# Transposes one unit later and a new order of work on three engines, in the forward stages of a four-layer kernel

## What is computed

```python
# layer 0: attention over channels
att = einsum('bcn,bdn->bcd', q, q)            # the Gram product
x = gamma * einsum('bcd,bdn->bcn', softmax(max(att) - att), q) + x
# layer 1: long convolution with a separable kernel hx (x) hy per channel
x = irfft2(rfft2(x) * rfft2(k)) + x * bias
# layer 2: Haar transform, two weighted channel mixes with soft thresholds
f1 = haar2d(x)
for i in range(2):
    f4 = einsum('bchw,oc->bohw', f1 * v[i], conv_w[i])
    acc = acc + sign(f4) * relu(abs(f4) - tau[i])
x = haar2d(acc, inverse=True) + x
# layer 3: a second long convolution like layer 1
```

## Time and profile before

| | |
|---|---|
| median of 3 runs | 6386.52 us (6386.07 to 6387.25) |
| the profiled execution | 6390.89 us, span 6389.1 us |
| PE busy | 5852.7 us (92%), weight loads 4944.5 us (77%) |
| DVE busy | 3975.6 us (62%) |
| ACT busy | 3883.7 us (61%) |
| POOL busy | 2526.3 us (40%) |
| chain that ended last | PE 85%, ACT 4%, DVE 3%, DMA 3%, issue 3% |
| DMA | 1216.97 MB, mean 190 GB/s |

### The profile page before, as it was taken

The page is one execution under the profiler, slowest core; times in us unless marked ns, Lnnn a source line. Parts: engine busy times, 40 slices in busy tenths (PEclk is TensorE's granted clock), DMA queues, the critical chain, the costliest instruction groups (busy, mean ns, idle before and its releaser), DMA issues.

```text
span 6389.1 us, 154198 instructions
## 1 busy us (share of the span) xinstructions
PE 5852.7 (92%) x47200; PEld 4944.5 (77%) x47200; DVE 3975.6 (62%) x6260; ACT 3883.7 (61%) x6105; POOL 2526.3 (40%) x2436
## 2 busy tenths in 40 slices
PE   5588589999999999999999999999999999999689
PEld 3277268888888888888888888878888887788579
DVE  1033158755886567755786568855786557766866
ACT  0222257755776667755776667755776657755865
POOL 0000045522553245522554245522554235533952
PEclk7599689999999999999999999999999999999789
DMA  6655666576666766666665866667665855534224
GB/s 183 208 179 175 208 191 206 185 238 207 206 207 191 249 186 206 202 214 215 204 207 184 253 191 207 197 215 229 194 206 179 253 173 166 166 116 138 76 85 129
DMA packets 770795, 1216.97 MB, mean 190 GB/s; under 512 B 78854, under 2 KB 475047, under 8 KB 770568
## 3 DMA queue, kind: packets, MB, share of 16 engines
q1 hardware_dynamic: 623112, 945.61, 50.0%
q10 hardware_dynamic: 147456, 268.50, 11.7%
HBM read 808.07 MB, written 405.73 MB: 190 GB/s over the span
## 4 chain that ended last, share of the span: by engine, by line
PE 85%; ACT 4%; DVE 3%; DMA 3%; issue 3%; ACTq 1%; SPq 1%; POOL 1%; DVEq 0%; POOLq 0%
PE ps L467 29%; PE ps L469 14%; PE ps L517 8%; PE ps L485 8%; PE ps L493 7%; PE ps L477 7%; PE ps L445 4%; PE ps L626 4%; PE ps L527 3%; DMA mixed<-x 2%; ACT x L802 1%; DMA pix<-in_x_pix 1%; DVE pix L1046 1%; DVE field L960 1%; ACT ps L847 1%
## 5 line engine op out<-in xcount | busy, mean ns | idle before, releaser
L1078 POOL TENSOR_TENSOR mag<-mag,sgn 128x512 f32<-128x512 f32 x896 | 1037.0, 1158 | 2154.8 <-ACT mag L733 2154.8
L467 PE MATMUL ps<-tab_a,img 128*128 128x256 f32 x4096 | 1288.9, 397 | 108.5 <-ACT mid L759 94.2
L1095 POOL TENSOR_TENSOR split_a<-field,split_a 128x512 fp32r<-128x512 f32 x512 | 650.7, 1271 | 1663.8 <-ACT split_a L785 1663.8
L467 PE MATMUL ps<-tab_b,mid 128*128 128x256 f32 x4096 | 1224.4, 381 | 0.0
L469 PEld LDWEIGHTS ps<-tab_a,img 128*128 128x128 f32 x4096 | 787.1, 192 | 110.1
L469 PEld LDWEIGHTS ps<-tab_b,mid 128*128 128x128 f32 x4096 | 778.9, 190 | 105.5
L467 PEld LDWEIGHTS ps<-tab_a,img 128*128 128x128 f32 x4096 | 663.7, 192 | 197.8 <-ACT mid L759 71.7
L469 PE MATMUL ps<-tab_a,img 128*128 128x128 f32 x4096 | 794.1, 276 | 0.0
L937 DVE TENSOR_TENSOR held<-ps,v_t 128x1024 f32<-128x1024 f32 x448 | 548.5, 1224 | 385.1 <-PE ps L517 385.1
L469 PE MATMUL ps<-tab_b,mid 128*128 128x128 f32 x4096 | 787.5, 274 | 0.0
L952 DVE TENSOR_TENSOR diff<-ps,tau_t 128x1024 f32<-128x1024 f32 x448 | 548.3, 1224 | 299.1 <-ACT ps L724 299.1
(11 more groups left out here) (92 smaller groups left out, 9394.3 us busy)
## 6 DMA issues: line engine op xcount, KB each, us to landing
pix<-in_x_pix SPq DMA_DIRECT2D x256, 512.0 KB, 4.4
mixed<-x ACTq DMA_DIRECT2D x512, 256.0 KB, 3.3
img<-mixed SPq DMA_DIRECT2D x512, 256.0 KB, 3.6
tab_a<-filt SPq DMA_DIRECT2D x1024, 128.0 KB, 3.0
tab_b<-filt SPq DMA_DIRECT2D x1024, 128.0 KB, 3.3
out<-res SPq DMA_DIRECT2D x512, 256.0 KB, 3.1
coef<-res ACTq DMA_DIRECT2D x496, 256.0 KB, 2.4
pix<-in_x_rows SPq DMA_DIRECT2D x128, 512.0 KB, 5.0
```

The source lines that it names most:

```text
L467: nc.tensor.matmul(o_ps, src[:, 0, H * half:H * half + H], tab[:, N - 1::-1], start=True, stop=False)
L1078: nc.gpsimd.tensor_tensor(mag[:, s], mag[:, s], sgn[:, s], ALU.mult).then_inc(c_mult, 1)
L1095: nc.gpsimd.tensor_tensor(split_a[:, 1], src, split_a[:, 0].bitcast(F32), ALU.subtract)\
```

## The change

On PE `turn` no longer closes the step of its own unit. It runs in the next step, behind the Gram and ahead of the row Toeplitz, for the unit before; it waits for the same count of field additions per unit as before. Also on PE, the column Toeplitz and `haar_fwd` change places, in all forward stages. On ACT, where the stage shrinks, the store moves from behind the high piece to between absolute and sign (in the last, draining steps and in the stage that doesn't shrink it stays). On DVE, where the stage shrinks, the low piece moves from the end of the step to behind held, and is of unit n-3 there, not n-2. No instruction is added or taken away.

```diff
--- before.py
+++ after.py
@@ -557,9 +557,9 @@
                         row_products(4, crows[j // 2], j % 2).then_inc(c_mm, 1)
 
                     def turn():
-                        src = crows[j // 2]
-                        pe.wait_ge(c_field, 64 * b + d + CR)
-                        row_turns(6, src, j % 2).then_inc(c_copy, 1)
+                        e = (j - 1) % 4
+                        pe.wait_ge(c_field, 64 * b + d - 1 + CR)
+                        row_turns(6, crows[e // 2], e % 2).then_inc(c_copy, 1)
 
                     def gram_four():
                         e = j - 1
@@ -573,6 +573,8 @@
                         products()
                     if gram and on[1] and not opening:
                         gram_four()
+                    if shrink and on[1] and not opening:
+                        turn()
                     if fwd and on[0]:
                         pe.wait_ge(img_in[j], 16 * (16 * (b + 1) + q) + 16)
                         pe.wait_ge(ftab_in[j], 32 * (16 * (b + 1) + q) + 32)
@@ -584,22 +586,22 @@
                         products()
                     if gram and on[1] and opening:
                         gram_four()
-                    if fwd and on[2]:
-                        pe.wait_ge(f_x1, n - 1 + CR)
-                        pe.wait_ge(f_lo, n - 2 + CR)
-                        haar_fwd(2, x1[:, j % 2]).then_inc(f_mm3, 1)
+                    if shrink and on[1] and opening:
+                        turn()
                     if fwd and on[1]:
                         d1 = j - 1
                         pe.wait_ge(f_mid, n + CR)
                         pe.wait_ge(f_x1, n - 1 + CR)
                         toeplitz(1, mid[:, d1 % 2], tab_b[:, d1 % 4]).then_inc(f_mm2, 1)
+                    if fwd and on[2]:
+                        pe.wait_ge(f_x1, n - 1 + CR)
+                        pe.wait_ge(f_lo, n - 2 + CR)
+                        haar_fwd(2, x1[:, j % 2]).then_inc(f_mm3, 1)
                     if fwd and on[3]:
                         pe.wait_ge(f_hi, n - 2 + CR)
                         pe.wait_ge(f_lo, n - 2 + CR)
                         pe.wait_ge(f_res, n - 3 + CR)
                         haar_halves(3, split_b, s_fwd_half).then_inc(f_mm4, 1)
-                    if shrink and on[0]:
-                        turn()
                     if gram and isinstance(q, int) and q == 16 and j == 0:
                         gram_edge(False).then_inc(gram_done, 1)
                     if fwd and shrink and isinstance(q, int) and q == 16 and j == 1:
@@ -719,10 +721,12 @@
                     n = f0 + 4 * q + j
                     m = 64 * b + 4 * q + j
 
-                    def absolute_and_sign():
+                    def absolute():
                         act.wait_ge(c_scaled, m + 1 + CR)
                         nc.scalar.activation(pair_of_banks(2), held[:].rearrange("p s n -> p (s n)"), ACT.Abs)\
                             .then_inc(c_abs, 1)
+
+                    def sign():
                         act.wait_ge(c_mult, 2 * m + CR)
                         nc.scalar.activation(sgn[:].rearrange("p s n -> p (s n)"),
                                              held[:].rearrange("p s n -> p (s n)"), ACT.Sign).then_inc(c_sign, 1)
@@ -732,9 +736,7 @@
                         act.wait_ge(c_pair, 2 * m + s - 1 + CR)
                         nc.scalar.activation(mag[:, s], diff[:, s], ACT.Relu).then_inc(c_relu, 1)
 
-                    if shrink and on[0]:
-                        absolute_and_sign()
-                        relu(0)
+                    draining = isinstance(q, int) and q == 16
 
                     def store():
                         d = j - 4
@@ -746,12 +748,18 @@
                         tile = last_res[d + 2] if draining and j >= 2 else res[:, d % 2]
                         act.dma_start(dst, tile.rearrange("p a n -> p (a n)")).then_inc(coef_out[d % 2], 16)
 
-                    draining = isinstance(q, int) and q == 16
+                    if shrink and on[0]:
+                        absolute()
+                    if fwd and shrink and on[4] and not draining:
+                        store()
+                    if shrink and on[0]:
+                        sign()
+                        relu(0)
                     if fwd and on[2]:
                         act.wait_ge(f_mm3, n - 1 + CR)
                         act.wait_ge(f_mm4, n - 2 + CR)
                         nc.scalar.activation(split_b[:, 0], halved(ps[:, 2, :]), ACT.Copy).then_inc(f_hi, 1)
-                    if fwd and on[4] and not draining:
+                    if fwd and not shrink and on[4] and not draining:
                         store()
                     if fwd and on[0]:
                         act.wait_ge(f_mm1, n + 1 + CR)
@@ -931,6 +939,11 @@
                     m = 64 * b + 4 * q + j
                     banks = pair_of_banks(2).rearrange(grouped, y=16)
 
+                    def low_piece(unit):
+                        dve.wait_ge(f_hi, unit + 1 + CR)
+                        nc.vector.tensor_tensor(split_b[:, 1], halved(ps[:, 2, :]), split_b[:, 0].bitcast(F32),
+                                                ALU.subtract).then_inc(f_lo, 1)
+
                     if shrink and on[0]:
                         dve.wait_ge(c_mm, m + 1 + CR)
                         dve.wait_ge(c_sign, m + CR)
@@ -938,6 +951,8 @@
                                                 table(v_t, q, j), ALU.mult).then_inc(c_scaled, 1)
                     if fwd and shrink and isinstance(q, int) and q == 16 and j == 3:
                         inverse_halves(64 * b, 0)
+                    if fwd and shrink and on[3]:
+                        low_piece(n - 3)
                     if fwd and on[4]:
                         d = j - 4
                         draining = isinstance(q, int) and q == 16
@@ -967,10 +982,8 @@
                         nc.vector.scalar_tensor_tensor(out=x1[:, d % 2], in0=img[:, d % 4],
                                                        scalar=bias1[:, bass.ds(4 * q + d, 1)], in1=halved(ps[:, 1, :]),
                                                        op0=ALU.mult, op1=ALU.add).then_inc(f_x1, 1)
-                    if fwd and on[2]:
-                        dve.wait_ge(f_hi, n - 1 + CR)
-                        nc.vector.tensor_tensor(split_b[:, 1], halved(ps[:, 2, :]), split_b[:, 0].bitcast(F32),
-                                                ALU.subtract).then_inc(f_lo, 1)
+                    if fwd and not shrink and on[2]:
+                        low_piece(n - 2)
                 quads(dve, 16, 4 if fwd else 1, step)
                 if shrink:
                     dve.wait_ge(c_field, 64 * b + 64 + CR)
```

## The result

The changed kernel took 6316.38 us in the median of four runs (6309.09 to 6321.73), the kernel before 6386.89: a ratio of 0.9888, interval 0.9871 to 0.9905. That is 70 us or 1.1% faster; the forecast was 6325 and 62 us. Its profiled execution took 6313.23 us with a span of 6311.4, against 6389.1.

What follows compares the result with a forecast made beforehand. With a Gram, PE's list and a ring through DVE's field addition both took 6.33 us a unit; without one, the ring bound. Gains of 18 + 36 + 8 = 62 us gave 6325 us, range 6300 to 6350 (0.68).

Steps and rivals of the forecast that it cites:

- The ring: Products, held, absolute, diff, field addition, transposes, next products: 6.33 us a unit; with transposes moved, 5.08 us, up to diff.
- PE's list with a Gram: Stages with a Gram: PE's work in the new order sums to 6.29 us a unit against 6.345, 18 us in all.
- Rival B: Only the stage without a Gram and the openings gain, 23 us, total 6363 us; chance 0.10.
- rival A: Tile changes are free in the new order: 72 to 133 us with a Gram, total 6242 us; chance 0.08.
- ACT: Store between absolute and sign: PE waits for mid without a Gram only, 5.75 us a unit there, 36 us gained.
- Rival C: ACT becomes the bound and mid comes late to the row Toeplitz: slower, total 6443 us; chance 0.07.
- The low piece: On DVE behind held: adds at most 0.06 us to a ring with over 1 us to spare; nothing.
- The exchange of Haar pass and column Toeplitz: On PE in every forward stage: same matmuls, same sum, neither moved piece in the ring without shrinking; nothing.
- DMA queues: SP's coefficient rows come in time, no image or table load moves, store issued some 2 us earlier; nothing.
- rival D: No change: the transposes' later count delays SP and coefficient rows come late for the products; 6380 us; chance 0.07.
- The opening: At each stage's opening the third products will need only diff: 1.2 us, seven times, 8 us.

## Why the prediction was right, and where it was off

**The ring.** Right. The period without a Gram fell by 0.58 with the whole change, by 0.38 when the transposes alone left the ring, and all but the transposes left it at 6.326. PE is busy 99.9% of the stage without a Gram, where the forecast asked for 97%, and no transpose waits for the field addition in the windows read.

**PE's list with a Gram.** Right in its kind, and short in size: 6.279 measured, 6.29 forecast, 6.345 before. It was charged with 0.05 a unit and 18 us; the stage shows 0.066, times 60 and six, 24 us, a third more. (The lower bound of this term, minus 130, should by its own numbers be minus 133 to 139.) Rival B, that only the stage without a Gram and the openings gain, fell with it. Summing starts of matmuls instead of idle times of loads is what kept the forecast from rival A's 72 to 133 us. The Trainium skill's sentence that a change of tiling mode drains TensorE ("TensorEngine Tiling (Array Packing)", Key Properties) names what these runs price: a fourth change costs 0.195 us a unit, and taking out one of every six gives back 0.13 for two units. That the array drains in that time, the traces don't show.

**ACT.** Right: mid late in the stage without a Gram, not in the others. The ring that I worked out gave 5.83 us and PE's list 5.67; I took 5.75 between them without a working of its own, so that 5.769 was measured is partly luck. The stage gained some 37 us after taking off the opening, where I had 36. Sign's start was forecast 4.73 us after the products, and came at 4.80 (1804.11 to 1808.91). Rival C (ACT as the bound with a Gram) did not come: mid ended 1.0 us before it was needed, where I had 0.84.

**The low piece: "Nothing".** This step failed. Its cover on DVE was there (diff still starts 2.51 after held), but what stands behind it is the store, and through it sign and mid: 0.11 us a unit without a Gram, 6 us. The sum was saved because the same 0.69 us was in the path of the store, and charged there to the store. So the price was in the sum, and its owner was wrong.

**The exchange of Haar pass and column Toeplitz: "Nothing".** This step failed too: 22 us hang on it in the last stage (388.3 against 366.1) once the low piece has moved, and it costs 6 us between the stages. Even the two moves together lose 6 us in the last stage, and 7 between the stages, to having left both in place. I compared the low piece's end with the Haar pass's new place alone.

**DMA queues.** Nothing, as forecast: PE waits for no coefficient rows in the windows 1590 to 1930 and 5210 to 5490 us, and rival D did not come.

**The opening.** Right: from the second to the third products it took 6.90 us before (1572.08 to 1578.98). After the change:

```profile
1560.12 2.08 PE L517 MATMUL ps<-chan_w,rows 64*128 64x128 f32 x16
...
1565.91 1.00 PEld L517 LDWEIGHTS ps<-chan_w,split_a 64*128 64x128 f32 x16 [1.39 <-issue]
1565.94 1.16 PE L517 MATMUL ps<-chan_w,split_a 64*128 64x128 f32 x16 [1.23 <-DVE diff L967]
```

That is 5.82, or 1.08 less, and the wait is now for diff, as said. The next unit took 5.99 before and 5.81 now, 0.18 less. Seven openings give 9 us.

Together 24 + 37 + 9 = 70 us, where the forecast had 18 + 36 + 8 = 62. The total is near because two terms were sized well and the third was 6 us short, and because the low piece's price sat in the store's path.

It is also near by luck, since the forecast had no term for the stretches between the stages. Five of the profiles build up the change one move at a time (us; one profile each):

| | the stage without a Gram | six stretches between stages |
|---|---|---|
| before | 404.6 | 1944.4 |
| and the transposes | 377.4 | 1949.9 |
| and the store | 359.8 | 1936.6 |
| and the low piece | 388.3 | 1937.5 |
| and the exchange: the changed kernel | 366.1 | 1943.4 |

Each stage with a Gram goes from 402.5 to 397.4 with the transposes and stays there. Between the stages the moves give and take up to 13 us, and happen to cancel.

## What to carry to other kernels

Before freeing an engine from a ring, write down its own list of work from start to start: where ring and list are equally long, as here with the Gram, opening the ring brings only what the new order of the list saves. When a group of small moves goes in together, take them out one by one: here two of the four repaired or harmed each other, and leaving both out was faster. Look at the stretches between stages too, not only at the steady part. Count changes of tile size as work, and put pieces of one size together, over two steps if need be.

## What the runs showed of the hardware that I had not expected

A pair of neighbouring pieces swapped on TensorE, with the same matmuls, cost 70 us of 6316, because one more change of tile size per unit costs 0.195 us at the upper clock. Gathering 16 + 16 Gram matmuls into 32 took 1.08 us, not 1.22. And the exchange of two neighbouring full-tile pieces, with equal periods inside the stages, went with a granted clock of 0.86 in place of 0.97 in the 50 us around a stage's end.
